# Attentions with heads of 16: where the products with the first 128 keys' values stand in TensorE's order

## The reference

```python
x = x + _L0_attn_ref(xn, ...) + _L0_ffn_ref(xn, ...)   # 32 heads of 16, causal
x = x + _L1_attn_ref(xn, ...) + _L1_ffn_ref(xn, ...)   # 32 heads of 16 on 8 key heads, causal
x = x + _L2_attn_ref(xn, ...) + _L2_ffn_ref(xn, ...)   # 32 heads of 128
x = x + _L3_attn_ref(xn, ...) + _L3_ffn_ref(xn, ...)   # 32 heads of 16 on 1 key head, causal
# each attention with heads of 16:
scores = jnp.einsum('bnth,bnsh->bnts', q, k) * (1.0 / math.sqrt(h))
scores = jnp.where(causal, scores, -jnp.inf)
attn = jax.nn.softmax(scores, axis=-1)
out = jnp.einsum('bnts,bnsh->bnth', attn, v)
```

## Time and profile before

| | |
|---|---|
| median of 3 runs | 2489.51 us (2488.51 to 2493.45) |
| profiled execution | 2488.93 us, its span in the trace 2487.2 us |
| TensorE busy | 2388.0 us, 96% of the span |
| VectorE, ScalarE, GpSimd busy | 64%, 44%, 23% |
| the 16 chunks of the first attention | from 334 to 452 us of the span |
| the middle and the last attention | until 829 us, and until 2453 us |

### The profile page before, as it was taken

How to read it: one execution, slowest core, us unless ns; L and a number is a source line. 1 busy time by engine, 2 the same in 40 slices (tenths; PEclk the granted TensorE clock), 3 DMA queues, 4 the chain that set the end, 5 groups by cost and what they waited for, 6 DMA issues and landing times. The chain is left out here.

```text
span 2487.2 us, 37936 instructions
## 1 busy us (share of the span) xinstructions
PE 2388.0 (96%) x12912; PEld 1918.9 (77%) x12912; DVE 1582.7 (64%) x2513; ACT 1105.3 (44%) x2158; POOL 572.2 (23%) x423
## 2 busy tenths in 40 slices
PE   5999999999989899999999999999999999999898
PEld 4777777688866678888888878888888886888666
DVE  5797468764378765544544477777777777543476
ACT  3333146532347442133333366666666654321573
POOL 2132021255231334044444300000000013441000
PEclk9999999999989999999999999999999999999999
DMA  3132175222243222234444432323223212332431
GB/s 89 42 123 85 40 134 99 35 47 46 45 102 70 38 38 40 52 117 145 141 150 139 144 94 80 93 84 93 61 74 93 75 40 38 51 51 44 93 66 47
DMA packets 406195, 195.14 MB, mean 78 GB/s; under 512 B 280392, under 2 KB 359728, under 8 KB 406078
## 3 DMA queue, kind: packets, MB, share of 16 engines
q1 hardware_dynamic: 404860, 191.53, 31.1%
q10 hardware_dynamic: 1218, 2.06, 0.3%
HBM read 129.85 MB, written 44.04 MB: 70 GB/s over the span
## 5 line engine op out<-in xcount | busy, mean ns | idle before, releaser
L616 PE MATMUL banks<-xn_hi,w_hi 128*128 128x512 f32 x1264 | 496.0, 392 | 10.1 <-ACT sgf L1156 7.1
L616 PE MATMUL banks<-xn_lo,w_hi 128*128 128x512 f32 x1264 | 492.7, 390 | 0.0
L616 PE MATMUL banks<-xn_hi,w_lo 128*128 128x512 f32 x1264 | 492.6, 390 | 0.0
L616 PEld LDWEIGHTS banks<-xn_hi,w_hi 128*128 128x128 f32 x1264 | 237.7, 188 | 61.1 <-DVE w_lo L604 7.2
L616 PEld LDWEIGHTS banks<-xn_hi,w_lo 128*128 128x128 f32 x1264 | 237.7, 188 | 49.9
L616 PEld LDWEIGHTS banks<-xn_lo,w_hi 128*128 128x128 f32 x1264 | 237.7, 188 | 48.0
L604 DVE TENSOR_TENSOR w_lo<-tw,w_hi 128x512 fp32r<-128x512 f32 (+2 forms) x136 | 116.0, 860 | 202.0 <-ACT w_hi L596 201.8
L2745 DVE TENSOR_SCALAR raw<-banks,cols 128x512 f32<-128x512 f32 x128 | 103.7, 810 | 180.3 <-ACT sq L2728 180.3
L2757 POOL TENSOR_TENSOR ssq<-ssq,sq 128x512 f32<-128x512 f32 x128 | 165.3, 1292 | 183.0 <-ACT sq L2728 183.0
L476 POOL TENSOR_TENSOR nat<-nat,wscale 128x512 f32<-128x512 f32 (+1 forms) x44 | 52.4, 1196 | 661.5 <-DMA nat<-in_L_ffn_w 661.5
L1277 POOL TENSOR_TENSOR h_lo<-sgf,h_hi 128x512 fp32r<-128x512 f32 (+1 forms) x94 | 128.3, 1369 | 327.4 <-ACT h_hi L1159 327.4
(11 more groups left out here) (290 smaller groups left out, 5556.3 us busy)
## 6 DMA issues: line engine op xcount, KB each, us to landing
qk_scratch<-raw SPq DMA_DIRECT2D x64, 512.0 KB, 3.0
qk_raw<-qk_scratch SPq DMA_DIRECT2D x64, 512.0 KB, 3.8
nat<-in_L_ffn_w SPq DMA_DIRECT2D x48, 256.0 KB
head_scratch<-stage SPq DMA_DIRECT2D x16, 512.0 KB, 3.2
st_qs<-st_hi SPq DMA_DIRECT2D x128, 64.0 KB, 2.0
nat<-in_L_attn_Wq SPq DMA_DIRECT2D x32, 256.0 KB
nat<-in_L_attn_Wk SPq DMA_DIRECT2D x32, 256.0 KB
nat<-in_L_attn_Wv SPq DMA_DIRECT2D x32, 256.0 KB
```

The source lines that it names most:

```text
L616: mm = nc.tensor.matmul(to[half][:, :], w[0:n, j, k * P:(k + 1) * P], r, start=first and k == 0 and x == 0, stop=last and k == len(rows) - ...
```

## The change

In the first attention `values(i, 0)` goes from behind `tops` to behind score block 1 of the round, ahead of shift block 5. In the joint attentions `out(g, 0)` is cut in two: its `kb` 0 part goes behind score block 0, ahead of shift blocks 10 and 11, and its `kb` 1 part stays. `out(g, 1)` stays whole. No instruction is added or taken away, and no wait changes its condition. The other engines' lists are unchanged.

```diff
-                def out(g, c):
-                    for kb in range(2) if 0 <= g < n_g else ():
+                def out(g, c, *kbs):
+                    for kb in kbs if 0 <= g < n_g else ():
                         joint_values(g, c, kb)
 
                 for g in range(-2, n_g):
                     for n in range(3):
                         shifts(g, 9 + n)
                         score(g + 2, n)
+                        if n == 0:
+                            out(g, 0, 0)
                     turn(g + 1, 1)
-                    out(g, 0)
+                    out(g, 0, 1)
...
                     turn(g + 2, 0)
-                    out(g, 1)
+                    out(g, 1, 0, 1)
...
                         shift(i, 3 + part)
                     if inside(i + 2):
                         scores(i + 2, part)
+                    if inside(i) and part == 1:
+                        values(i, 0)
                 if inside(i + 1):
                     tops(i + 1)
                 if inside(i):
-                    values(i, 0)
                     values(i, 1)
```

## The result

| | before | after |
|---|---|---|
| median of the runs side by side | 2489.51 us (5 runs) | 2503.09 us (5 runs, 2502.0 to 2504.96) |
| ratio, 95% interval | | 1.0049 (1.0035 to 1.0063) |
| profiled execution, its span | 2488.93, 2487.2 us | 2502.0, 2500.2 us |

The change made the kernel slower by 0.49%, 12.2 us of 2489.5 (8.7 to 15.7). The medians themselves stand 13.6 us apart. The forecast was 2506.0 us in a range of 2495.6 to 2510.

The account below looks back on a forecast made before the run. TensorE's order sets the pace, with slack in ScalarE's exponential-copy chain; 6.4 + 5.1 - 0.6 + 0.3 + 2.2 + 3.1 = 16.5 us on 2488.9, median 0.6 above, gives 2506.0 us, range 2495.6 to 2510.

Parts of the forecast that it names:

- V0: TensorE's products with the first 128 keys' values, four waves per chunk; moved ahead of the last shift or last two.
- D: Price of V0 in its new place, switches to and from waves included: 1.10 us, delaying the last exponential by as much.
- The bound with free switches: V0's place: the two switches between full-width products and waves cost nothing, D = 0.88 us, 9.7 us in all.
- the one with a dearer leaving: V0's place: leaving the waves costs twice what the rows show, D = 1.21 us, 19.9 us in all.
- E + 1.79: Next chunk's first shift, counted from the last exponential's start E, waits for ScalarE's query copy; E + 2.43 before, first attention.
- V1: TensorE's products with the other keys' values, four waves in 0.55 us; forecast to wait for the exponential ending at E + 0.60.
- Steady rounds: Chunks 0 to 13, first attention: 14 x 0.46 = 6.4 us; pairs 1 to 5, two joint attentions: 10 x 0.51 = 5.1 us.
- Ends: Last rounds without score blocks: 2 x 1.10 = 2.2 us in the first attention, 4 x 0.78 = 3.1 us in the joint ones.
- First rounds: V0 fills DMA holes between shifts: last attention's first round gains 0.59 us, the middle one's loses 0.26 us.
- Faster: Rival: V0's waves run beside the full-width products around them, D much under 0.88 us; 2479 to 2486 us, chance 0.09.
- No change: Rival: switches free and V1 runs while the copy's tail is still hidden; 2492 to 2494 us, chance 0.13.
- The rival of the clock: Longer waits in the last rounds drop TensorE to its lower clock, adding 2 to 5 us; 2508 to 2511, chance 0.04.

Follow-up runs that it names:

- split_behind: Against the kernel before: last shift left in place, the two sets of values split by score block 3 in steady rounds of all attentions; 2493.47 us, ratio 1.0028.
- late_shift: Against the kernel before, first attention only: score blocks 2 and 3 moved ahead of the last shift, values whole; 2497.65 us, ratio 1.0044.
- first_only: Against the kernel before: the change in the first attention alone; 2498.52 us, ratio 1.0053.
- steady_only: Against the kernel before: the change only in rounds with score blocks, the last two rounds of each attention as before; 2498.09 us, ratio 1.0051.
- before_again: The kernel before, unedited, traced a second time and compared with itself; 2489.22 us, ratio 1.0001.
- score_first_a: Against the kernel before: score block ahead of its shift block in each round's first half, first attention only; 2487.73 us, ratio 0.9990.

## Why the prediction was right

**Price of V0, D = 1.10 us.** It measured 1.22 less 0.12, 1.10, in the first and in the middle attention. The parts hold too: entering took 0.22 us for the forecast 0.21 (402.09 to 402.31), the steps between the waves 0.67 for 0.68 (402.31 to 402.98), the last wave 0.33 for 0.33 (402.98 to 403.31). The bound with free switches fell with `split_behind`; the one with a dearer leaving fell with the 0.33.

**The chain.** E + 1.79 and E + 1.78 came out to the hundredth, and `late_shift`, which has the late shift without V0's move, shows the same E + 1.79. The margin by which the copy decides was thinner than I wrote: TensorE was ready for the shift at E + 1.69, not at E + 1.56. Nearly all of this is V1, which started at E + 0.65 and not at E + 0.54: it waited for the exponential, and 0.05 us more behind its end (404.73 to 404.78). My sum for E + 1.56 had left this wait out, though the sentence ahead of it names it. The forecast of E + 1.79 did not hang on it, but the copy decides by 0.10 us and not by 0.23.

**Steady rounds.** Forecast +0.46 and +0.51; measured 7.60 to 7.63 against 7.13, which is +0.47 to +0.50 and +0.48 in the mean, and 13.69 to 13.73 against 13.17, +0.52 to +0.56. Over 14 and 10 rounds that is 6.7 instead of 6.4 us and 5.3 instead of 5.1.

**Ends.** Forecast 2.2 us for the first attention, measured 2.2 (`first_only` less `steady_only`). Forecast 0.78 for each of four places in the joint ones, measured 0.71 and 0.74 at the two that I read.

**First rounds.** Here the terms (-0.6 and +0.3) cannot be read. The DMA hole of 1.71 us comes and goes from trace to trace at the same code: `first_only`, whose last attention is that of before, shows 0.82 us there, and this row:

```profile
2365.29 0.35 PE L2311 MATMUL banks<-st_ks,st_qs 96*128 96x256 f32 x1 [0.82 <-DMA st_qs<-st_hi]
```

In the last attention the first pair's distance, 13.92 us before, is 13.09 after, 13.08 in `first_only` and 14.19 in `before_again`. A term from one such row was worth no more than the spread of 1 us that these show. Over the first third of a stage the means of the traces named above differ by -1.0 us in the middle attention and -0.8 in the last, inside a spread of 1.6 and 2.1 at the same code: the sum of -0.3 is neither borne out nor refuted.

**Sum.** Forecast 16.5 us; the stages gave 16.0 and 13.6 in two pairs of traces, the ratios 12.2 (8.7 to 15.7) and 13.7 us (10.2 to 17.2). Where the traces can be read without the chance of a start, the terms hold: +8.8 to +8.9 us in the first attention for the forecast 8.6, and +4.0 in each joint one from its fifth copy on for 4.1 (five rounds of 0.51 and two ends of 0.78). What is left of the distance to the medians lies in the first rounds, and in what no edit touches: the openings (329.1 to 334.3 us in the traces of one code) and the granted clock. How it is shared out stays open. That the median came within 3 us of 2506.0 is in that part luck; that rounds and ends cost what they cost is not.

**The rivals of the forecast.** "Faster" needed D under 0.59: it is 1.10, so nothing of V0's 0.88 us was hidden by full-width products beside it. "No change" needed free switches: they cost 0.24 us a pair of them. The rival of the clock was about the last rounds, and there it was granted in full in all three attentions of the changed kernel, in spite of the longer waits:

```profile
443.00:457.80 14.80, 11.82 (x132) 7.73 (x125) 10.00 (x20) 10.91 (x20) 1.46 (x2) 1.00 0.15 24
...
820.00:841.50 21.50, 15.82 (x187) 9.63 (x186) 14.69 (x36) 14.29 (x27) 7.42 (x8) 1.00 0.20 34
2450.00:2465.90 15.90, 13.36 (x167) 7.82 (x165) 9.61 (x19) 11.52 (x23) 2.68 (x4) 1.00 0.01 2
```

Of the Trainium skill's rule (TensorEngine Tiling (Array Packing), Key Properties), that changing the tiling mode drains the engine, `split_behind` shows what the two added changes cost here: 0.24 us in a round in which the work is the same. The trace agrees in that a change costs time; that it is a drain no run shows.

## What to carry to other kernels

In an order written by hand, ask of each block not only what it waits for but which chain it covers: V0 behind the last shift cost TensorE nothing extra there and hid, with V1 and a score block, 1.65 us of ScalarE's exponential and copy; ahead of it, the same products delayed that chain and left it bare. To price a move, add what lies ahead of the chain's head to its start and compare the chain's end, row by row, with the start that it releases; the slack (0.6 us here) is the whole of what may be given away. Price the switches between waves and full-width products as well: here they were half of a round's loss. And where one trace's span jumps by 5 us at the same code, count the change in the distances of its own rounds.

## What the runs showed of the hardware that I had not expected

In steady and last rounds TensorE started 0.14 us behind the end of ScalarE's copy of 1.02 us over 32 partitions (405.78 to 405.92; 0.14 or 0.15 in each kernel here that waits there), but 0.05 us behind the end of its exponential of 0.60 us over 128 (404.73 to 404.78). It is not the copy itself that makes the difference: behind the first copy of each attention the shift starts 0.05 or 0.06 us after the end, in the kernel before at 340.83, 725.62 and 2349.47. These first shifts wait for no exponential as well, as the later ones do by their code; no run tests whether that is the reason.

In two executions of the same code the granted clock of the stretch from 2000 to 2338 us was 1.00 and 0.98, and the stretch between the middle and the last attention, in which it lies, was 5.9 us longer in the second. The first 37 to 38 us of the middle attention, with the same code there, were granted 0.72 in `before` and `before_again`, 0.81 in `score_first_a` and 0.82 in `first_only`.
